# Bias products as row tiles, the small attention's softmax as one block, DMAs moved to ScalarE's queue, new instruction orders

## Chip, cores and metric

One core of a Trainium2 chip runs the kernel. The metric is the device time of one execution in microseconds (us); lower is better. TensorE (PE), VectorE (DVE), ScalarE (ACT), GpSimd (POOL) and SyncE (SP, which only issues DMAs here) each work through an instruction list of their own and meet at semaphores.

## The reference

Two transformer layers act on `x` of shape 64 x 64 x 256 (samples, rows of a sample, 256 features), with a context `ctx` of the same shape and a mask over the context's rows:

```python
x = x + L0_xattn(layernorm(x), ctx, Wq, bq, Wk, bk, Wv, bv, Wo, bo)     # 8 heads of 8 channels over 256 positions, rotary
x = x + L0_ffn(layernorm(x), gate_w, gate_b, val_w, val_b, out_w, out_b)
x = x + L1_xattn(layernorm(x), ctx, mask)                               # plain attention of 64 rows on 64 rows, no weights
x = x + L1_ffn(layernorm(x), w_gate_up, w_proj)
# L0_ffn: bit_linear(silu(bit_linear(x, gate_w) + gate_b) * (bit_linear(x, val_w) + val_b), out_w) + out_b;
#   bit_linear rounds each row to 8 bits and the weights to -1, 0, 1 times their mean magnitude
# L1_xattn: scores = x ctx^T / 16, masked, softmax, times ctx; rows of a sample with an all-masked context get 0
# L1_ffn: weights in groups of 64 rounded to -1, 0, 1 times the group's mean magnitude; silu(gate) * up, RMS norm, w_proj
```

In L0's attention the 64 rows of a sample are the channels, and the 256 features are the positions.

## The kernel before

**Pairs and stages.** Two samples are stacked to the 128 partitions; there are 32 such pairs. Every pair passes the same steps, named by short kinds. Projection stage (P): `xP`, `cP` (loads), `bsP mvP rsP xnP` (layer norm), `proj0 proj1` (query and key products), `pc r1 r2 rot` (rotary), `hi lo` (split into two fp16 parts), `kq` (six DMAs that lay the parts out in `KQ`, 32 partitions for each of four groups of heads), `v vst`. Attention (A): for each of 16 heads `S` (scores, TensorE, 31 rows), `mx` (row maximum, DVE), and, once all 16 maxima are there, `mxp` (TensorE transposes them), `mxc` (ACT copies them to `mxs`), `md` (a DMA writes them into row 31 of `KQ`), then for each head `T` (transposed scores minus maximum, TensorE, 32 rows), `E` (exponential, ACT) and, for each four heads, `pv`. `u ov sg rc d1 or om y x1` divide by the sum, project and add. FFN of L0 (B): `bsB mvB rsB xnB`, `amB sxB xr xq rq qT` (8-bit rounding and a DMA transpose), `Bg Bv` (two halves of 512 columns each), `tB aB hB amH sx hr hq ht Bd x2`. L1's attention (D): `bsD mvD rsD xnD xcT xcTc sc wx pD rs pT pTc ro x3`. FFN of L1 (C): `bsC mvC rsC xnC xh xl xT Cg Cu th aC hC sq hh hl hT Cd ms x4 st`.

**Order.** The steps run as a software pipeline. `ORDER` holds one written list for each engine; `S6:0` in iteration `it` is head 6 of pair `it + 0`, `Bg0:-3` works on pair `it - 3`, `proj0:2` on pair `it + 2`. An engine does its list in order, so a step that waits holds up all behind it. From the first step of a pair to its last are some ten iterations. Kinds in `ONCE` (the weights: `c ab ra qa rn cl qb fx tn tc` and `gm gv fr ct bs br mn val`) run once, in the iteration their number names, which puts them in the first iterations.

**PSUM.** `psS` and `psT` are two banks each for `S` and `T`, used in turn. Four more banks, `psW`, are shared by everything else: `BANKS` lists who takes each bank in turn, and `READER` names the step that must have read a bank before the next taker writes it. TensorE's `S` and `T` use row tiles: each works on the 32 partitions of its group, and four neighbours in the list are in four groups. `pv` uses column tiles, the rest the whole array.

**Places the change touches.** In `Bg` and `Bv` the bias is a third product into the same bank, of the whole array, from a 128-row tile `brow` with six rows that are not zero (L493). L960 (`wx`) takes the maximum and L657 (`pD`) the exponential of each sample's 64 x 64 block of the scores apart; L965 and L966 (`rs`, DVE) turn the sum into a factor. L732 and L737 on POOL centre and scale a row, among them `xnP`. SP issues every DMA: the weights (L299 to L320), and `md` (L350), which stands in SP's list after `kq` (L347), `cB`, `xT` (L390) and `hT` (L395, a DMA transpose that waits for `hl` of POOL):

```python
elif name == "md":
    after_apart(sp, "mxc", p)
    sp.dma_start(KQ[p % DEEP][31::32, 1, :, :], mxs[:]).then_inc(S["md"], 16)
```

Of the kernel before, what the change touches and what calls it, by code (L numbers as in the profile page):

```python
# [69 lines left out]
ORDER = {  # L70
    "pe": """Cd0:-7 tn4:-3 T4:-1 S6:0 S7:0 T5:-1 tn5:-3 pT:-5 Cd1:-7 ro:-5 pv0:-1 S8:0 T6:-1 T7:-1 S9:0 proj0:2 Bg0:-3
           T8:-1 S10:0 T9:-1 S11:0 pv1:-1 Bv0:-3 gm:0 tn1:-2 S12:0 S13:0 T10:-1 T11:-1 Bd:-4 Bg1:-3 S14:0 T12:-1
           S15:0 T13:-1 Bv1:-3 y:-2 proj1:2 mxp:0 T14:-1 S0:1 T15:-1 S1:1 pv2:-1 tn2:-2 Cg0:-5 pv3:-1 S2:1 T0:0 S3:1
           T1:0 xcT:-4 tn3:-2 tn0:-1 Cu0:-5 Cg1:-5 S4:1 T2:0 S5:1 T3:0 sc:-4 v:2 Cu1:-5""",
    "dve": """mx5:0 aC1:-6 bsP:3 cl1:-1 rc:-2 rs:-5 hC1:-6 ra2:1 mx6:0 x4:-7 mx7:0 ct1:-3 ct0:-2 x3:-5 mvP:3 ct2:-3
           bs:-1 ra1:2 mx8:0 mx9:0 bsC:-5 cl0:1 r1:2 mvC:-5 mx10:0 mx11:0 aB0:-3 mx12:0 mx13:0 val:1 fx2:-2 x2:-4
           hB0:-3 bsD:-4 mx14:0 mvD:-4 mx15:0 fx0:-1 gv:0 aB1:-3 bsB:-2 hB1:-3 mvB:-2 mx0:1 amH:-3 ra0:3 mx1:1
           fx1:-1 cl2:-1 sx:-3 mx2:1 mx3:1 aC0:-5 amB:-2 hC0:-5 sxB:-2 wx:-4 mx4:1""",
    "act": """th1:-6 pD:-5 xr:-3 pTc:-5 xq:-3 E4:-1 hh0:-6 E5:-1 tc4:-3 hi:1 hh1:-6 E6:-1 E7:-1 fr0:-1 fr2:-2 c1:21
           tc5:-3 tB0:-3 E8:-1 E9:-1 sq0:-6 E10:-1 xh:-5 E11:-1 ab2:0 ab0:1 u0:-1 tB1:-3 E12:-1 E13:-1 x1:-2 tc1:-2  # L80
           rn2:0 mxc:0 E14:-1 E15:-1 mn:1 pc:2 sq1:-6 c0:24 ab1:1 fr1:-1 th0:-5 tc2:-2 u1:-1 E0:0 hr0:-3 rn1:1 E1:0
           rn0:2 xcTc:-4 c2:4 hr1:-3 tc0:-1 tc3:-2 E2:0 E3:0 vst:2""",
    "pool": """rq:-3 ms:-7 rot:1 qa2:0 qa0:2 xb:-3 qb2:-2 hl0:-6 lo:1 rsC:-5 xnC:-5 qb0:-1 xl:-5 qa1:1 qb1:-1 om:-2
           hl1:-6 rsP:3 rsD:-4 xnD:-4 xnP:3 rsB:-2 xnB:-2 r2:2 hq0:-3 hq1:-3""",
    "sp": """xP:4 ov:-1 st:-7 cP:3 ht:-3 d1:-1 qT:-2 sm:3 or:-1 kq:2 br:0 cB:-3 w0:9 xT:-4 hT:-5 md:1 xA:0 sg:0""",
}
# [966 lines left out]
```

## Time and profile before

| | |
|---|---|
| time, median of 3 runs | 869.65 us (865.7 to 870.27) |
| the profiled execution's own time | 870.44 us |
| its span, first to last instruction | 868.6 us |
| busy in the span: PE, DVE, ACT, POOL | 757.4, 760.5, 687.1, 650.2 us (87, 88, 79, 75%) |
| granted TensorE clock, mean of the span | 0.935 of full |

Busy time is an average over a start, a long even part and an end. The start and the end have idle engines; what a step costs in the even part is read there, from the distance of one iteration's landmark to the next's. The landmark used below is `mxc` (L600), which runs once in each iteration.

### The profile page before, as it was taken

The page shows a single profiled execution, that of the slowest core. Times are in us where ns is not written, and L with a number is a line of the kernel's source. Part 1 is how long each engine was busy: PE and PEld are TensorE (multiplying, and loading weights), DVE is VectorE, ACT ScalarE, POOL GpSimd, SP SyncE. Part 2 cuts the span into 40 slices and gives each one's busy share as a digit, 9 for nine tenths or more (in the row PEclk, how much of TensorE's full clock was granted, in tenths as well). Part 3 has the DMA queues.
Part 4 walks back from the last instruction along what each step waited for, and adds up shares of the span by engine and source line. Part 5 has one row for each costly group of instructions (what it writes and reads, how often), then busy time and mean ns, then how long its engine had stood idle before and what let it go on. Part 6 is the DMA issues. An engine that isn't in the chain of part 4 may idle for free. (4 is left out here: it accounts for less than half of the span.)

```text
span 868.6 us, 21831 instructions
## 1 busy us (share of the span) xinstructions
PE 757.4 (87%) x6713; PEld 394.0 (45%) x6804; DVE 760.5 (88%) x1714; ACT 687.1 (79%) x1469; POOL 650.2 (75%) x1108
## 2 busy tenths in 40 slices
...
GB/s 327 70 38 27 51 68 75 70 102 101 96 112 97 100 108 106 104 105 111 108 104 105 101 110 105 104 106 104 101 96 112 97 102 96 92 81 105 83 43 72
DMA packets 210859, 84.67 MB, mean 97 GB/s; under 512 B 152748, under 2 KB 209708, under 8 KB 210744
## 3 DMA queue, kind: packets, MB, share of 16 engines
...
## 5 line engine op out<-in xcount | busy, mean ns | idle before, releaser
L876 DVE TENSOR_REDUCE mx<-psS 128x2 f32<-128x512 f32 x512 | 333.8, 679 | 26.6 <-PE psS L441 24.7
L595 ACT ACTIVATE prob<-psT 128x512 f32<-128x512 f32 x512 | 288.4, 603 | 32.1 <-PE psT L449 31.7
L441 PE MATMUL psS<-KQ 31*128 31x256 f16 x1024 | 132.7, 285 | 20.3 <-DVE mx L876 17.8
L463 PE MATMUL psW<-prob,vst 128*32 128x256 f32 x2048 | 143.4, 400 | 0.3 <-ACT prob L595 0.3
L528 PE MATMUL psW<-guT,xT 128*128 128x512 bf16 x482 | 124.4, 391 | 21.4 <-DMA xT<-stage 19.0
L449 PE MATMUL psT<-KQ 32*128 32x256 f16 x1024 | 113.4, 280 | 11.8 <-DMA KQ<-mxs 8.8
L776 POOL TENSOR_TENSOR stage<-stage 128x512 f16<-128x512 f32 x64 | 74.1, 1158 | 18.7 <-ACT stage L678 18.4
L441 PEld LDWEIGHTS psS<-KQ 31*128 31x128 f16 x1024 | 37.9, 93 | 103.4 <-DVE mx L876 77.3
L463 PEld LDWEIGHTS psW<-prob,vst 128*32 128x32 f32 x2048 | 55.0, 112 | 63.7 <-issue 32.4
L528 PEld LDWEIGHTS psW<-guT,xT 128*128 128x128 f16 x512 | 48.2, 100 | 74.9 <-issue 37.2
L762 POOL TENSOR_TENSOR hqB<-wide,rnd 128x512 bf16<-128x512 f32 x64 | 65.9, 1040 | 17.0 <-ACT wide L639 16.8
L490 PE MATMUL psW<-tern,xqT 128*128 128x512 bf16 x195 | 63.6, 382 | 16.4 <-DMA xqT<-xqB 10.7
L537 PE MATMUL psW<-pT,stage 128*128 128x256 bf16 x512 | 67.8, 278 | 5.2 <-DMA stage<-stage 5.2
L634 ACT ACTIVATE stage<-psW,sB 128x512 f32<-128x512 f32 x64 | 44.8, 701 | 31.5 <-PE psW L493 31.5
L537 PEld LDWEIGHTS psW<-pT,stage 128*128 128x128 f16 x512 | 50.2, 102 | 20.8 <-ACT vst L615 8.2
L977 DVE SCALAR_TENSOR_TENSOR stage<-stage,psW 128x512 f32<-128x512 f32 x64 | 43.6, 681 | 18.4 <-ACT stage L670 18.1
L670 ACT ACTIVATE stage<-psW 128x512 f32<-128x512 f32 x64 | 39.6, 619 | 21.1 <-PE psW L528 21.1
L449 PEld LDWEIGHTS psT<-KQ 32*128 32x128 f16 x1024 | 33.5, 93 | 50.1 <-issue 24.9
L476 PE MATMUL psW<-cP,wsm 128*128 128x256 f32 x128 | 46.7, 450 | 6.7 <-POOL xnP L737 4.6
L985 DVE SCALAR_TENSOR_TENSOR stage<-stage,hsc,psW 128x512 f32<-128x512 f32 x64 | 47.6, 743 | 3.1 <-PE psW L528 2.9
L493 PE MATMUL psW<-brow,xqT 128*128 128x512 bf16 x128 | 48.6, 380 | 0.1
L930 DVE SCALAR_TENSOR_TENSOR wide<-stage,psW 128x512 f32<-128x512 f32 x64 | 43.3, 677 | 5.3 <-ACT stage L634 5.3
...
## 6 DMA issues: line engine op xcount, KB each, us to landing
...
oR<-rden_d SPq DMA_DIRECT2D x128, 32.0 KB
...
```

The costliest lines, as they stand in the source:

```text
L441: m = nc.tensor.matmul(psS[:, n % 2, T * k:T * k + T], KQ[p % DEEP][r, 1, g, 128 * k:128 * k + 128], KQ[p % DEEP][r, 0, g, :], start=True, ...
L449: m = nc.tensor.matmul(psT[:, n % 2, T * k:T * k + T], KQ[p % DEEP][r, 0, g, 128 * k:128 * k + 128], KQ[p % DEEP][r, 1, g, :], start=True, ...
L463: m = nc.tensor.matmul(bank[32 * j:32 * j + 32, :], vst[p % DEEP][:, k, 4 * n + j, :], prob[:, (4 * n + j) % 8, k, :], start=(k == 0), sto ...
L490: nc.tensor.matmul(bank, xqT[:, k, :], (gT if kind == "Bg" else vT)[:, k, 512 * n:512 * n + 512], start=(k == 0), stop=False)
L493: m = nc.tensor.matmul(bank, xqT[:, NK, :], brow[:, int(kind == "Bv"), 512 * n:512 * n + 512], start=False, stop=True)
L528: m = nc.tensor.matmul(bank, xT[:, NK * part + k, :], w[:, k, :], start=(k == 0 and part == 0), stop=(k == NK - 1 and part == 1))
L537: m = nc.tensor.matmul(psW[:, BANK["Cd0"], 0:T], hT[:, 8 * part + c, :], pT[:, c, :], start=(c == 0 and part == 0), stop=(c == 7 and part ...
L595: m = nc.scalar.activation(flat(prob[:, n % 8, :, :]), psT[:, n % 2, :], ACT.Exp, scale=float(HC) ** -0.5)
L762: m = nc.gpsimd.tensor_tensor(hqB[:, h], hrB[:, h], rnd[:].broadcast_to([P, 512]), ALU.subtract)
L776: m = nc.gpsimd.tensor_tensor(hhl[:, 1, n, :], hC[:, n, :], hhl[:, 0, n, :], ALU.subtract)
L876: m = nc.vector.tensor_reduce(mx[:, p % 2, :, 4 * (n % 4) + n // 4], psS[:, n % 2, :].rearrange("p (c s) -> p c s", c=NK), AX.X, ALU.max)
L985: m = nc.vector.scalar_tensor_tensor(out=hC[:, n, :], in0=aC[:, n, :], scalar=hsc[:, 1:2], in1=psW[:, BANK[f"Cu{n}"], :], op0=ALU.mult, op ...
```

## The change

- `Bg` and `Bv` lose the third product. Four new steps, `bg0 bg1 bv0 bv1`, open their banks with the bias instead (six rows, row tiles of the four groups, 512 columns); `brow` now lies in groups at partitions 0, 32, 64, 96, and `rq` writes the row factors into four places.
- `sc` gets one more product (`own` and `other`, 2 rows, 128 columns) that pushes the two off-diagonal blocks far down; `wx` and `pD` then work on all 128 x 128 at once.
- `rs` moves from DVE to POOL (a power and a product). `xnP` moves from POOL (centre, scale) to ACT (one activation with scale and bias); POOL's `rsP` gains a product for the bias.
- `md` and the six 1 MB weight loads are issued from ACT's queue; each load has a semaphore of its own.
- POOL's weight products `qa`, `qb` run in four pieces each.
- `ORDER` and `BANKS` are new for all engines.

```diff
 ORDER = {
-    "pe": """Cd0:-7 tn4:-3 T4:-1 S6:0 S7:0 T5:-1 tn5:-3 pT:-5 Cd1:-7 ro:-5 pv0:-1 S8:0 T6:-1 T7:-1 S9:0 proj0:2 Bg0:-3
-           T8:-1 S10:0 T9:-1 S11:0 pv1:-1 Bv0:-3 gm:0 tn1:-2 S12:0 S13:0 T10:-1 T11:-1 Bd:-4 Bg1:-3 S14:0 T12:-1
-           S15:0 T13:-1 Bv1:-3 y:-2 proj1:2 mxp:0 T14:-1 S0:1 T15:-1 S1:1 pv2:-1 tn2:-2 Cg0:-5 pv3:-1 S2:1 T0:0 S3:1
-           T1:0 xcT:-4 tn3:-2 tn0:-1 Cu0:-5 Cg1:-5 S4:1 T2:0 S5:1 T3:0 sc:-4 v:2 Cu1:-5""",
+    "pe": """ro:-5 pv0:-1 T6:-1 S8:0 T7:-1 bg0:-3 S9:0 proj0:2 Bg0:-3 S10:0 T8:-1 T9:-1 S11:0 pv1:-1 Bd:-4 bv0:-3
+           S12:0 bv1:-3 S13:0 T10:-1 bg1:-3 T11:-1 Bv0:-3 Bg1:-3 Bv1:-3 S14:0 T12:-1 S15:0 T13:-1 y:-2 proj1:2 mxp:0
+           T14:-1 S0:1 S1:1 T15:-1 pv2:-1 Cg0:-5 pv3:-1 tn0:0 tn4:-4 Cg1:-5 xcT:-4 gm:1 S2:1 T0:0 S3:1 T1:0 Cu0:-5
+           v:2 sc:-4 S4:1 T2:0 S5:1 T3:0 tn2:-2 Cu1:-5 tn1:-1 tn3:-3 tn5:-4 Cd0:-6 pT:-4 S6:1 T4:0 S7:1 T5:0 Cd1:-6""",
...
     "act": (after)
+           ... mxc:0 E14:-1 E15:-1 md:0 pc:2 th0:-5 u1:-1 tc1:-2 xnP:3 rn1:1 tc0:0 th1:-5 xcTc:-4 E0:0 mn:3 E1:0 hr0:-3
+           vst:2 xr:-2 E2:0 pD:-4 c0:14 E3:0 xq:-2 hr1:-3 ab0:2 tc2:-2 c1:3""",
...
-    "sp": """xP:4 ov:-1 st:-7 cP:3 ht:-3 d1:-1 qT:-2 sm:3 or:-1 kq:2 br:0 cB:-3 w0:9 xT:-4 hT:-5 md:1 xA:0 sg:0""",
+    "sp": """xP:4 cP:3 st:-8 sm:9 ov:-1 d1:-1 qT:-2 ht:-3 or:-1 kq:2 xT:-4 cB:-3 xA:0 hT:-5 br:-1 sg:0""",
...
-BANKS = ("tn4 pT ro Bg0 tn1 Bg1 pv2 Cg1",
-         "Cd0 proj0 gm Bd Bv1 tn2 tn3 Cu0 v",
-         "pv0 y mxp Cg0 tn0 Cu1",
-         "tn5 Bv0 proj1 xcT sc")
+BANKS = ("bv1 tn0 Cg1 v tn1 tn5 Cd0",
+         "proj0 Bd y mxp Cg0 tn4 gm Cu1",
+         "ro bg0 bg1 pv2 Cu0 tn3",
+         "pv0 bv0 proj1 xcT sc tn2 pT")
...
+                    elif kind in ("bg", "bv"):
+                        after_dma(pe, "qT", p)
+                        if p == 0:
+                            after_dma(pe, "br", 0, 6)
+                        r = slice(32 * (2 * (kind == "bv") + n), 32 * (2 * (kind == "bv") + n) + 6)
+                        m = nc.tensor.matmul(bank, xqT[r, NK, :], brow[r, :], start=True, stop=False)
                     elif kind in ("Bg", "Bv"):
...
                         for k in range(NK):
-                            nc.tensor.matmul(bank, xqT[:, k, :],
-                                             (gT if kind == "Bg" else vT)[:, k, 512 * n:512 * n + 512],
-                                             start=(k == 0), stop=False)
-                        m = nc.tensor.matmul(bank, xqT[:, NK, :], brow[:, int(kind == "Bv"), 512 * n:512 * n + 512],
-                                             start=False, stop=True)
+                            m = nc.tensor.matmul(psW[:, BANK[f"{kind.lower()}{n}"], :], xqT[:, k, :],
+                                                 (gT if kind == "Bg" else vT)[:, k, 512 * n:512 * n + 512],
+                                                 start=False, stop=(k == NK - 1))
...
+                        m = nc.tensor.matmul(bank[:, 0:P], own[:], other[:], start=False, stop=True)
...
+            for i, (raw, part) in enumerate(((stage[:, 3, :], gu_w[0:HID, :]), (late[0], gu_w[HID:2 * HID, :]))):
+                nc.scalar.dma_start(raw.rearrange("p (r d) -> p r d", r=8), part.rearrange("(r p) d -> p r d", p=P))\
+                    .then_inc(S[f"w1_{i}"], 16)
+            ... (p_w, gate_wT, val_wT and out_wT in the same way)
...
+                    elif kind == "md":
+                        after(act, "mxc", p)
+                        nc.scalar.dma_start(KQ[p % DEEP][31::32, 1, :, :], mxs[:]).then_inc(S["md"], 16)
+                        continue
...
+                    elif kind == "xnP":
+                        after(act, "rsP", p)
+                        after(act, "proj", p - 1, 1)
+                        m = nc.scalar.activation(xnP[:], xP[:], ACT.Identity, scale=rsP[:, 1:2], bias=nmP[:])
...
-                        for b in range(2):
-                            h = slice(CH * b, CH * b + CH)
-                            m = nc.scalar.activation(pD[h, h], psW[h, BANK["sc"], h], ACT.Exp, bias=sD[h, 1:2],
-                                                     accum_out=sD[h, 2:3])
+                        m = nc.scalar.activation(pD[:], psW[:, BANK["sc"], 0:P], ACT.Exp, bias=sD[:, 1:2],
+                                                 accum_out=sD[:, 2:3])
...
+                        for g in range(0, WB // 64, 8):
+                            m = nc.gpsimd.tensor_tensor(q[:, g:g + 8, :], (w if kind == "qa" else q)[:, g:g + 8, :],
+                                                        by[:, g:g + 8, :], ALU.mult)
...
+                        if kind == "rsP":
+                            inner(2, m)
+                            m = nc.gpsimd.tensor_scalar(nmP[:], mv[:, 0:1], rs[:, 1:2], -1.0, ALU.mult, ALU.mult)
...
+                    elif kind == "rs":
...
+                        inner(1, nc.gpsimd.tensor_tensor(sD[:, 3:4], sD[:, 2:3], mone[:], ALU.pow))
+                        m = nc.gpsimd.tensor_tensor(sD[:, 4:5], sD[:, 3:4], valid[:, p:p + 1], ALU.mult)
...
-                        for b in range(2):
-                            h = slice(CH * b, CH * b + CH)
-                            m = nc.vector.tensor_reduce(sD[h, 1:2], psW[h, BANK["sc"], h], AX.X, ALU.max, negate=True)
+                        m = nc.vector.tensor_reduce(sD[:, 1:2], psW[:, BANK["sc"], 0:P], AX.X, ALU.max, negate=True)
```

## Rows read from the trace of the kernel before

**Rows 1.** Windows: start:end, length, busy (instructions) of each engine, clock, DMA share, GB/s.
```profile
250.00:700.00 450.00, 430.81 (x4080) 227.26 (x4137) 433.02 (x1017) 392.01 (x880) 378.34 (x665) 1.00 0.43 105
764.20:868.60 104.40, 72.67 (x474) 39.66 (x477) 54.53 (x134) 54.35 (x129) 62.73 (x120) 0.88 0.34 79
```

**Rows 2.** Tile `mxs`, then the timeline: start, length, instruction [idle before it, releaser].
```profile
L600 ACT ACTIVATE mxs<-psW x32: 373/373/374, 55.7 to 764.2; 16x256 f16<-16x256 f32 x32
...
145.12 0.37 ACT L600 ACTIVATE mxs<-psW 16x256 f16<-16x256 f32 x1 [0.61 <-PE psW L455]
...
443.47 0.37 ACT L600 ACTIVATE mxs<-psW 16x256 f16<-16x256 f32 x1 [0.61 <-PE psW L455]
...
467.78 0.37 ACT L600 ACTIVATE mxs<-psW 16x256 f16<-16x256 f32 x1 [0.61 <-PE psW L455]
...
490.06 0.37 ACT L600 ACTIVATE mxs<-psW 16x256 f16<-16x256 f32 x1 [0.61 <-PE psW L455]
...
764.19 0.37 ACT L600 ACTIVATE mxs<-psW 16x256 f16<-16x256 f32 x1 [0.48 <-PE psW L455]
```

**Rows 3.** Timeline of SP's queue beside two of those iterations.
```profile
442.93 2.85 SPq L395 DMA_TRANSPOSE stage<-stage  x1
445.82 0.63 SPq L350 DMA_DIRECT2D KQ<-mxs  x1
...
468.25 0.63 SPq L350 DMA_DIRECT2D KQ<-mxs  x1
```

**Rows 4.** Waits of TensorE, 250 to 700 us: total us, times, longest.
```profile
PE psT L449 <- DMA KQ<-mxs: 5.7, 8, 1.8
...
PEld psT L449 <- DMA KQ<-mxs: 8.7, 10, 2.1
```

**Rows 5.** DVE by line, 250 to 700 us (busy, mean ns | idle before), and its timeline.
```profile
L876 DVE TENSOR_REDUCE mx<-psS 128x2 f32<-128x512 f32 x315 | 205.9, 678 | 9.4 <-PE psS L441 8.6
...
L960 DVE TENSOR_REDUCE sD<-psW 64x1 f32<-64x64 f32 x38 | 8.2, 217 | 4.9 <-PE psW L512 4.4
...
752.08 0.11 DVE L965 RECIPROCAL sD<-sD 128x1 f32<-128x1 f32 x1
...
752.43 0.75 DVE L985 SCALAR_TENSOR_TENSOR stage<-stage,hsc,psW 128x512 f32<-128x512 f32 x1
```

**Rows 6.** Timeline of TensorE: a bias product, and a group of four tiles behind it.
```profile
412.36 0.38 PE L490 MATMUL psW<-tern,xqT 128*128 128x512 bf16 x1
412.58 0.38 PE L493 MATMUL psW<-brow,xqT 128*128 128x512 bf16 x1
412.89 0.28 PE L449 MATMUL psT<-KQ 32*128 32x256 f16 x1
...
413.23 0.42 PE L463 MATMUL psW<-prob,vst 128*32 128x256 f32 x4
```

**Rows 7.** Timeline of ACT: from the first softmax block to the next step.
```profile
406.60 0.30 ACT L657 ACTIVATE pD<-psW,sD 64x64 f32<-64x64 f32 x1
...
407.43 0.51 ACT L624 ACTIVATE xrB<-xnB,sB 128x256 f32<-128x256 f32 x1
```

**Rows 8.** Waits of ACT, 250 to 700 us.
```profile
ACT stage L634 <- PE psW L493: 18.9, 20, 1.9
```

**Rows 9.** POOL by line, 250 to 700 us.
```profile
L737 POOL TENSOR_TENSOR xnP<-ceP,rsP 128x256 f32<-128x256 f32 x20 | 12.3, 613 | 1.6
...
L724 POOL TENSOR_TENSOR rsD<-rsD,mhalf 128x1 f32<-128x1 f32 x20 | 11.0, 549 | 1.6
...
L722 POOL TENSOR_TENSOR rsC<-mvC,eps 128x1 f32<-128x1 f32 x20 | 3.8, 189 | 27.1 <-DVE mvC L897 27.1
```

**Rows 10.** Timeline of the start: SP's queue and DVE.
```profile
10.53 7.27 SPq L337 DMA_DIRECT2D xP<-in_x  x1
...
24.30 0.43 DVE L890 BATCH_NORM_STATS2 stP<-xP 128x6 f32<-128x256 f32 x1 [8.04 <-DMA xP<-in_x]
...
38.35 0.61 PE L441 MATMUL psS<-KQ 31*128 31x256 f16 x4 [1.65 <-DMA KQ<-hl]
```

More of the change, by code:

```diff
@@ L56 @@
 PARTS = {**{k: NH for k in ("S", "mx", "T", "E")}, "pv": NG,
-         **{k: 2 for k in ("proj", "u", "Bg", "Bv", "aB", "tB", "hB", "Cg", "Cu", "th", "aC", "hC", "sq",
+         **{k: 2 for k in ("proj", "u", "bg", "bv", "Bg", "Bv", "aB", "tB", "hB", "Cg", "Cu", "th", "aC", "hC", "sq",
                            "hh", "hl", "Cd", "hr", "hq")}}
 ONCE = {"c": 3, "ab": 3, "gm": 1, "gv": 1, "bs": 1, "br": 1, "mn": 1, "val": 1, "ra": 3, "qa": 3, "rn": 3, "cl": 3,
-        "qb": 3, "fx": 3, "fr": 3, "ct": 3, "tn": 6, "tc": 6, "w0": 1, "sm": 1}
+        "qb": 3, "fx": 3, "fr": 3, "ct": 3, "tn": 6, "tc": 6, "sm": 1}
 PARTS.update(ONCE)
-INNER = {"xnP": 1, "xnB": 1, "xnD": 1, "xnC": 1, "rsP": 1, "rsB": 1, "rsC": 1, "rsD": 1, "sxB": 1,
+INNER = {"xnB": 1, "xnD": 1, "xnC": 1, "rsP": 2, "rsB": 1, "rsC": 1, "rsD": 1, "sxB": 1,
          "sx": 2, "ms": 3, "rs": 1, "rq": 3, "rn": 1, "fr": 1, "ra": 3, "fx": 1, "gv": 4,
@@ L68 @@
 DEEP = 3
-SET_POOL, SET_DVE = 10, 2 * DEEP + 2
+SET_POOL, SET_DVE = 12, 2 * DEEP + 2
 ORDER = {
-    "pe": """Cd0:-7 tn4:-3 T4:-1 S6:0 S7:0 T5:-1 tn5:-3 pT:-5 Cd1:-7 ro:-5 pv0:-1 S8:0 T6:-1 T7:-1 S9:0 proj0:2 Bg0:-3
-           T8:-1 S10:0 T9:-1 S11:0 pv1:-1 Bv0:-3 gm:0 tn1:-2 S12:0 S13:0 T10:-1 T11:-1 Bd:-4 Bg1:-3 S14:0 T12:-1
-           S15:0 T13:-1 Bv1:-3 y:-2 proj1:2 mxp:0 T14:-1 S0:1 T15:-1 S1:1 pv2:-1 tn2:-2 Cg0:-5 pv3:-1 S2:1 T0:0 S3:1
-           T1:0 xcT:-4 tn3:-2 tn0:-1 Cu0:-5 Cg1:-5 S4:1 T2:0 S5:1 T3:0 sc:-4 v:2 Cu1:-5""",
[L75 to L84, printed above, removed]
-    "sp": """xP:4 ov:-1 st:-7 cP:3 ht:-3 d1:-1 qT:-2 sm:3 or:-1 kq:2 br:0 cB:-3 w0:9 xT:-4 hT:-5 md:1 xA:0 sg:0""",
-}
```

101 lines of the change are left out of this document (51 added, 50 removed).

## The prediction

> **What bounds the kernel now.** I first split the run by the landmark `mxc`. It runs first at 55.7 us, is at 145.12 in its fifth turn and at 764.19 in its last [rows 2]. From the fifth to the last are 27 iterations in 619.1 us, 22.93 us each. Ahead lie four iterations that also carry the weights' one-time work (89.4 us for the four), and behind the last landmark an end of 104.4 us [rows 1]. So 619 of 868.6 us are an even part, and what a change is worth is mostly 27 times what it does to the iteration.
>
> Second, who is busy in the even part. A window of 450 us holds 19.6 iterations (450 / 22.93). DVE is busy 433.0 / 19.6 = 22.1 us of each, PE 22.0, ACT 20.0, POOL 19.3 [rows 1]. Two engines are nearly full, at the full granted clock. PE's figure flatters, since modelled ends overlap; DVE's is what its instructions take.
>
> Third, whether iterations are alike. They are not: 443.47 to 467.78 is 24.31 us, 467.78 to 490.06 is 22.28 us [rows 2]. SP's queue tells them apart. `mxs` was written at 443.5, but its DMA (L350) was issued at 445.82, because SP sat in the transpose ahead of it (L395) from 442.93; in the good iteration the DMA went out at 468.25, half a us after `mxs` [rows 3]. The four groups of T0 cannot start without it: TensorE waited for this DMA 5.7 + 8.7 = 14.4 us in the window [rows 4], 0.73 us in each iteration, and TensorE's list is in order, so the next `S`, and through it DVE, wait too. The mean of 22.93 is thus 22.28 plus 0.65 of lateness. In the good iteration DVE is 99% busy: DVE, with PE close behind, is the floor, and the lateness of `md` is what lies on top.
>
> **The change, part by part, in us for each iteration.**
>
> *`md` on ACT.* It leaves the queue with `kq`, `xT` and `hT` ahead of it. In ACT's new list it stands behind E14 and E15, so it goes out some 1.5 us after `mxs`; but between `mxp` and T0 the new PE list has Cg1 and xcT as well as T14, S0, S1, T15, two `pv` and Cg0, so T0 comes later. I take off most of the lateness: 0.65 down to 0.2, since `kq`, `xT` and `hT` stay in one queue behind POOL. Bounds: 0 and 0.65.
>
> *PE.* A bias product of 512 columns takes 0.22 (412.36 to 412.58), four are 0.88. A group of four row tiles, eight products of 256 columns, takes 0.34 with the change of mode behind it (412.89 to 413.23) [rows 6]: its tiles run side by side. The new bias products have six rows and stand among such groups. `bg0` is in the partitions of S8 and follows it, 0.22. `bv0 S12 bv1 S13 T10 bg1 T11` put three of them beside the others: three of the four row groups have one bias more to do, and the run is longer by one, 0.22. So 0.88 becomes 0.44. The `own` product has a quarter of 512 columns: +0.06. Counting changes between whole array, row tiles and column tiles, the old list has 20 in an iteration and the new one 21 (Cg1 now stands behind pv3); one costs about 0.1, what 412.58 to 412.89 has above 0.22 [rows 6]. Net: -0.28. Bounds: all biases hidden, -0.72; no overlap, +0.16.
>
> The Trainium skill (TensorEngine Tiling (Array Packing), Key Properties) says that changing the tiling mode drains TensorE, which speaks against a list with more changes; the trace agrees, at about 0.1 each [rows 6]. By that rule alone the change would cost 0.1 an iteration; by the rows it is already in the sum.
>
> *DVE.* Two maxima of 64 columns take 217 ns each, 512 columns take 678 [rows 5], so a column costs 1.03 ns and one maximum over 128 takes 0.28 in place of 0.43: -0.15. `rs` goes: from L965 to the next step is 752.08 to 752.43 [rows 5], -0.35. Net -0.50. Bounds: the merged maximum no cheaper, -0.35; its wait for `sc` (4.4 us in the window, 0.22 each [rows 5]) gone as well, -0.72.
>
> *ACT.* The two softmax blocks with their accumulator reads take 0.83 (406.60 to 407.43) [rows 7]. One takes half, and its 64 more columns 0.07 (0.51 for 256 columns against 0.30 for 64 [rows 7]): -0.34. `xnP` is 0.51 by the row of the same size. The DMA issue takes SP 0.63 [rows 3]; ACT's queue isn't in the trace, so from 0 (E15 runs meanwhile) to 0.63. ACT goes from 20.0 to between 20.2 and 20.8, under the floor; I take 0.63 in full and find cover for it in ACT's 2.96 idle.
>
> *POOL.* Off go the two passes of `xnP`, 0.61 each, with a handover of 0.08 behind each (1.6 us over 20): -1.4. On come one small step in `rsP` and the two of `rs`: 0.19 + 0.19 + 0.55 [rows 9] and three handovers: +1.2. POOL stays at some 19.1 [rows 9], with 1.4 idle at `rsC` alone (27.1 us in the window). `rs` must be there for `x3` in the next iteration; beside it run `pT`, `pTc` and `ro`. The pieces of `qa` and `qb` are in the first iterations only. All this counts as nothing; if POOL's cover is gone, `hl` is late, then `hT`, then Cd0.
>
> *Start.* SP's issue of the second pair's `xP` lasted 7.27, from 10.53, behind the weights; it landed for DVE at 24.30 after 8.04 of waiting, and `r1` of the first pair stands behind that in DVE's list, so S0 came at 38.35 [rows 10]. With the weights on another queue this can shrink by up to 8. But the new ACT list has the mask row, two casts of weights, and now `xnP` itself ahead of the first rotary step, all in one queue, and `gm` stands ahead of S2 and waits for all three sums of ACT. I take -1, bounds -8 and +5.
>
> The Trainium skill (DMA: Bandwidth & Descriptors, Issuing engines are not separate DMA queues) holds that transfers of all issuing engines interleave on the same 16 DMA engines and that a second one saves only issue time. By it the 6 MB delay the second `xP` as before, and the start gains 0 to 1; that no load arrives sooner can't be read from the trace of before.
>
> *End.* Without `S` and `T` beside them the bias tiles need changes of mode of their own, four in three late iterations, +1; `rs` is longer but runs beside `ro`; no `md`. I take 0, bounds ±3.
>
> **Sum.** Floor of PE: 22.28 - 0.28 = 22.00. Floor of DVE: 22.28 - 0.50 = 21.78. The later one counts, 22.00, plus 0.2 of lateness: 22.2. That is 0.73 less than 22.93, times 27 = 19.7 us. With 1 from the start: 870.44 - 20.7 = 849.7. The profiled execution was 0.8 above the median of the runs, so the prediction is **849 us**.
>
> **Rivals.**
> - *Better than that:* no lateness, DVE's floor of 21.8, a start 5 shorter: 1.13 x 27 + 5 = 35.5, 834 us. For it: all three fullest places are relieved. Against: PE's new order has a mode change more. 9 in 100.
> - *The lateness stays:* SP's queue still holds `kq`, `hT` and `xT` in turn, so T4 or Cd0 takes T0's place; only PE's 0.28 counts: 0.28 x 27 = 7.6, 862 us. It needs `hT` to wait for POOL as at 442.93 [rows 3] and TensorE to have nothing else. 15 in 100.
> - *No change:* small gains eaten, for example by TensorE waiting at `bg0` for `x3` to free the bank of `ro`, with only pv0, T6, S8 and T7 between (before, proj0 too): 0.65 lost at this wait leaves the iteration at 22.9. 866 to 873 us. 10 in 100.
> - *Slower:* ACT becomes the bound. Its 20.8 of work plus today's idle of (450 - 392.0) / 19.6 = 2.96 make 23.76. A third of the idle is one wait for a product just being made (18.9 us in the window, 0.96 an iteration [rows 8]), which a denser list need not shorten, and `md` stands between two steps that feed TensorE. (23.76 - 22.93) x 27 = 22: 892 us at worst, about 880 if half the issue is covered. It decides once ACT's idle stays above 2.1. 14 in 100.
>
> The forecast itself, 838 to 860, gets 52 in 100.
>
> **Numbers.** What the measurement of this kernel can tell from no change is about 0.5%, 4.3 us. Faster by more: forecast, better, and lateness stays, 0.76. Within: 0.10. Slower: 0.14. The range takes the better case's 834, and at the top goes past no change to 872; it leaves out the slower case and the far end of the start's bounds.
>
> **What would show it.** Right: landmarks 22.0 to 22.4 apart with no long ones among them; waits of T0 for `KQ<-mxs` near nothing; DVE near 21.6 of work an iteration; row-tile bias products starting within 0.05 of their neighbours; ACT under 21. Wrong: a new long wait of TensorE (`bg0` on `x3`, S0 on `kq`, Cd0 on `hT`), ACT idle still near 3 with landmarks above 22.9, or a first landmark after 60 us.

## The result, and the profile after

The changed kernel takes **856.31 us** (median of four runs, 853.29 to 858.92), the kernel before 869.86 beside it: a ratio of 0.985, 95% interval 0.981 to 0.990. That is faster by 13.6 us, where the forecast was 20.7. The profiled execution took 853.29 us, with a span of 851.4.

Head of the page, then two windows of the kernel after: start:end, length, busy time and instructions of PE, PEld, DVE, ACT and POOL, granted clock, DMA share, GB/s; they answer to [rows 1].
```profile
span 851.4 us, 22001 instructions
...
PE 750.5 (88%) x6836; PEld 395.3 (46%) x6836; DVE 740.3 (87%) x1618; ACT 695.6 (82%) x1437; POOL 647.9 (76%) x1160
...
250.00:700.00 450.00, 442.64 (x4335) 239.38 (x4332) 443.38 (x1000) 415.71 (x899) 393.67 (x713) 1.00 0.48 109
...
750.00:851.40 101.40, 69.98 (x431) 36.92 (x430) 46.75 (x107) 48.00 (x110) 62.16 (x120) 0.86 0.35 75
```

The landmark `mxc` of the kernel after, by its tile and by ACT's timeline. It answers to [rows 2]; the fifth is at 148.56.
```profile
L595 ACT ACTIVATE mxs<-psW x32: 373/373/374, 60.1 to 744.2; 16x256 f16<-16x256 f32 x32
...
148.56 0.37 ACT L595 ACTIVATE mxs<-psW 16x256 f16<-16x256 f32 x1 [0.61 <-PE psW L441]
...
392.63 0.37 ACT L595 ACTIVATE mxs<-psW 16x256 f16<-16x256 f32 x1
...
414.58 0.37 ACT L595 ACTIVATE mxs<-psW 16x256 f16<-16x256 f32 x1
...
744.25 0.37 ACT L595 ACTIVATE mxs<-psW 16x256 f16<-16x256 f32 x1
```

| part of the span | before | after | difference | forecast |
|---|---|---|---|---|
| up to the first landmark | 55.7 | 60.1 | +4.4 | -1 for both |
| the first four iterations | 89.4 | 88.4 | -1.0 | |
| the 27 even ones | 619.1 | 595.7 | -23.4 | -19.7 |
| behind the last landmark | 104.4 | 107.15 | +2.7 | 0 |
| span | 868.6 | 851.4 | -17.2 | -20.7 |

(The profiled executions differ by more than the medians, 17.2 against 13.6; each is read against its own kind.) The even part gained more than forecast, and start and end gave 6 us back. An iteration is now 22.06 us (595.7 / 27), against 22.93. Its median is 21.95, as 392.63 to 414.58 shows, against 22.28 in a good iteration before. So of the 0.65 us of lateness 0.11 are left (0.54 x 27 = 14.6 us), and the floor, the length of an iteration that nothing holds up, is 0.33 lower (0.33 x 27 = 8.9 us). The window now holds 450 / 22.06 = 20.4 iterations: DVE is busy 21.7 us in each, PE 21.7, ACT 20.4, POOL 19.3. ACT is idle 1.7 by this count, which leaves out the issuing of DMAs: `md`'s, some 0.55, lies in those 1.7.

TensorE's waits of the kernel after from 250 to 700 us (us in total, times, longest). `KQ<-mxs` of [rows 4] doesn't appear at all; what is new is a wait of `pT` (L504) for `pD`, 14.8 us or 0.7 in each iteration.
```profile
PEld psS L427 <- DVE mx L897: 21.9, 55, 0.5
...
PEld psW L504 <- ACT pD L658: 9.8, 18, 0.7
...
PE psW L504 <- ACT pD L658: 5.0, 15, 0.5
```

Timeline of the kernel after: `md` (ACTq, L598) goes out 0.45 after `mxs`, 0.2 **ahead** of the transpose of `hT` (SPq, L381); T0 (L435) follows 4.2 later with no wait. In [rows 3] the transpose stood ahead of `md`. Over the 20 iterations of the window `md` goes out 0.45 to 0.98 after `mxs` (the prediction had 1.5), and ahead of the transpose in 19. It lands 1.9 to 4.0 us after its issue. T0 comes 4.2 to 4.3 after the issue, against 2.3 to 2.8 in the iterations of before without a wait, so the longer way to T0 is used too: six of the 20 landings came later than 2.8.
```profile
393.08 0.56 ACTq L598 DMA_DIRECT2D KQ<-mxs  x1
393.29 2.64 SPq L381 DMA_TRANSPOSE stage<-stage  x1
...
397.24 0.28 PE L427 MATMUL psS<-KQ 31*128 31x256 f16 x1
397.25 0.28 PE L435 MATMUL psT<-KQ 32*128 32x256 f16 x1
```

Timeline of TensorE, kernel after: the bias products (L474, six rows) among row tiles, to be read beside [rows 6].
```profile
409.98 0.39 PE L474 MATMUL psW<-brow,xqT 6*128 6x512 bf16 x1
409.98 0.28 PE L427 MATMUL psS<-KQ 31*128 31x256 f16 x1
409.99 0.38 PE L474 MATMUL psW<-brow,xqT 6*128 6x512 bf16 x1
...
410.20 0.27 PE L435 MATMUL psT<-KQ 32*128 32x256 f16 x1
410.22 0.38 PE L474 MATMUL psW<-brow,xqT 6*128 6x512 bf16 x1
...
410.59 1.47 PE L479 MATMUL psW<-tern,xqT 128*128 128x512 bf16 x6
```
Two bias products start within 0.01 us of each other and of a product of `S`. The group with three of them lasts 0.61 us (409.98 to 410.59), against 0.34 for one without [rows 6]: the three cost 0.27 together, where three products over the whole array cost 0.66 before.

Groups of instructions of the kernel after, 250 to 700 us (total and mean ns of one, then idle before it).
```profile
L979 DVE TENSOR_REDUCE sD<-psW 128x1 f32<-128x128 f32 x20 | 5.3, 266 | 0.0
...
L643 ACT ACTIVATE xnP<-xP,nmP,rsP 128x256 f32<-128x256 f32 x20 | 12.0, 602 | 0.0
L658 ACT ACTIVATE pD<-psW,sD 128x128 f32<-128x128 f32 x20 | 7.2, 358 | 0.0
L658 ACT ACTIVATION_READ_ACCUMULATOR pD<-psW,sD 128x1 f32 x20 | 4.0, 199 | 0.0
...
L805 POOL TENSOR_TENSOR sD<-sD,mone 128x1 f32<-128x1 f32 x20 | 11.0, 549 | 0.0
```
These are new shapes, and each can be set against its estimate: 266 ns for the merged maximum (0.28), 0.36 + 0.20 for the merged softmax (0.49), 0.60 for `xnP` (0.51), 0.55 for POOL's power (0.55, as its like in [rows 9]).

Start of the kernel after, to be read beside [rows 10]: SP's queue, the first step of ACT that needs the mask row (L573), the second pair's statistics (L911), and the first `S`.
```profile
7.71 10.76 SPq L319 DMA_DIRECT2D mrow<-in_mask  x1
19.21 5.88 SPq L319 DMA_DIRECT2D mrow<-in_mask  x1
25.13 8.71 SPq L326 DMA_DIRECT2D xP<-in_x  x2
...
26.77 1.91 ACT L573 ACTIVATE mneg<-mrow 2x2048 bf16<-2x2048 uint8 x1 [14.46 <-DMA mrow<-in_mask]
27.49 0.43 DVE L911 BATCH_NORM_STATS2 stP<-xP 128x6 f32<-128x256 f32 x1 [12.72 <-DMA xP<-in_x]
...
42.86 0.61 PE L427 MATMUL psS<-KQ 31*128 31x256 f16 x4 [2.90 <-DMA KQ<-hl]
```
The two small mask rows now hold SP's queue for 16.6 us (3.9 and 1.3 before), ahead of the second pair's `xP`; ACT waits 14.46 for them. The first `S` comes 4.5 us later than before, and so does the first landmark.

### The profile page after: what moved, and what is told of

Same layout as the page of the kernel before. It is cut to its first block and busy times, and to the rows that moved or that the text cites. A ratio compares the mean times of both kernels' runs of the same rounds, so it can differ in the third digit from the quotient of the medians.

```text
span 851.4 us, 22001 instructions
## 1 busy us (share of the span) xinstructions
PE 750.5 (88%) x6836; PEld 395.3 (46%) x6836; DVE 740.3 (87%) x1618; ACT 695.6 (82%) x1437; POOL 647.9 (76%) x1160
## 5 line engine op out<-in xcount | busy, mean ns | idle before, releaser
L897 DVE TENSOR_REDUCE mx<-psS 128x2 f32<-128x512 f32 x512 | 331.1, 678 | 15.1 <-PE psS L427 14.3
L516 PE MATMUL psW<-guT,xT 128*128 128x512 bf16 x512 | 135.5, 390 | 13.6 <-DMA xT<-stage 11.9
L427 PE MATMUL psS<-KQ 31*128 31x256 f16 x1024 | 129.1, 284 | 12.7 <-DVE mx L897 9.3
L435 PE MATMUL psT<-KQ 32*128 32x256 f16 x1024 | 119.8, 279 | 3.2 <-ACT prob L590 2.2
L516 PEld LDWEIGHTS psW<-guT,xT 128*128 128x128 f16 x512 | 41.2, 99 | 84.8 <-issue 52.2
L776 POOL TENSOR_TENSOR hqB<-wide,rnd 128x512 bf16<-128x512 f32 x64 | 66.5, 1040 | 14.3 <-ACT wide L638 14.3
L479 PE MATMUL psW<-tern,xqT 128*128 128x512 bf16 x256 | 68.5, 392 | 0.0
L462 PE MATMUL psW<-cP,wsm 128*128 128x256 f32 x128 | 47.4, 455 | 22.3 <-DMA cP<-in_ctx 19.1
L990 DVE SCALAR_TENSOR_TENSOR stage<-stage,psW 128x512 f32<-128x512 f32 x64 | 43.6, 682 | 21.3 <-ACT stage L671 20.2
L633 ACT ACTIVATE stage<-psW,sB 128x512 f32<-128x512 f32 x64 | 44.0, 688 | 20.1 <-PE psW L479 18.5
L435 PEld LDWEIGHTS psT<-KQ 32*128 32x128 f16 x1024 | 40.9, 93 | 33.3 <-ACT prob L590 20.5
L604 ACT COPY uA<-psW 128x512 f32<-128x512 f32 x64 | 37.5, 586 | 21.7 <-PE psW L449 21.7
L770 POOL TENSOR_TENSOR r<-pc,tab 128x512 f32<-128x512 f32 x32 | 40.7, 1272 | 17.3 <-ACT pc L609 17.3
```

The lines of the kernel that those rows point to most:

```text
L427: m = nc.tensor.matmul(psS[:, n % 2, T * k:T * k + T], KQ[p % DEEP][r, 1, g, 128 * k:128 * k + 128], KQ[p % DEEP][r, 0, g, :], start=True, ...
L435: m = nc.tensor.matmul(psT[:, n % 2, T * k:T * k + T], KQ[p % DEEP][r, 0, g, 128 * k:128 * k + 128], KQ[p % DEEP][r, 1, g, :], start=True, ...
L462: m = nc.tensor.matmul(bank[:, T * f:T * f + T], wqk[:, j, :], (cP, xnP)[f][:], start=True, stop=True)
L479: m = nc.tensor.matmul(psW[:, BANK[f"{kind.lower()}{n}"], :], xqT[:, k, :], (gT if kind == "Bg" else vT)[:, k, 512 * n:512 * n + 512], sta ...
L516: m = nc.tensor.matmul(bank, xT[:, NK * part + k, :], w[:, k, :], start=(k == 0 and part == 0), stop=(k == NK - 1 and part == 1))
L633: m = nc.scalar.activation(tB[:, 512 * n:512 * n + 512], psW[:, BANK[f"bg{n}"], :], ACT.Tanh, scale=sB[:, p % 2, 4:5])
```

## The experiments

Each was run beside the kernel before on the same chip; ratios are to it. `b_slack`, `a_md_sp_early`, `a_pt_late` and `a_start` ran on another chip than the rest, where the kernel before took 867.68 us (869.63 and 869.95 in the other two groups), so they are compared with the others by ratios as well. Landmark figures are distances over the 27 even iterations of the profiled execution, the mean where nothing else is said. A second run of the changed kernel, in the first group, gave the level for comparisons: 856.47 us, 0.985 (0.981 to 0.990), mean 22.15. Its expectation:

> The changed kernel once more, as the yardstick of this group on the same chip. Both theories: 853 to 859 us. Its landmarks (the copy of the maxima, once an iteration) were 21.95 us apart in the undisturbed iterations, 22.06 in the mean; the time moved between 853 and 859 from run to run, and the profile of this run may show where.

### Which part of the move takes the lateness away

**`md` on ACT alone, in the kernel before** (`b_md_act`).
```diff
-  E14:-1 E15:-1 mn:1           (ACT)       xT:-4 hT:-5 md:1 xA:0   (SP)
+  E14:-1 E15:-1 md:0 mn:1      (ACT)       xT:-4 hT:-5 xA:0        (SP)
```


> The kernel before, with one thing changed: the DMA of the maxima is issued from ACT's queue, behind E15. Theory 1 (the DMA was late because of what stood ahead of it in SP's queue, 0.65 us an iteration): landmarks 22.3 apart with none over 22.7, waits of T0 for it down from 14.4 us in the window 250 to 700 to under 7 (the old list has less work between the maxima and T0 than the new one, so some stays), time 853 to 860. Rival A (SP's queue and POOL hold up the iteration in another place, and this DMA only shows it): landmarks stay near 22.9, time 865 to 873. Rival B (the issue of 0.6 us on ACT costs what it saves): T0's wait gone, but the landmarks evenly at 22.7 or more.

868.8 us, 0.999 (0.995 to 1.002): nothing. The mean distance is 22.92. `md` now always leaves 0.41 us after `mxs` begins, and T0 still waits for it. Timeline and waits of this kernel:
```profile
352.13 2.18 SPq L392 DMA_TRANSPOSE stage<-stage  x1
...
353.27 0.37 ACT L597 ACTIVATE mxs<-psW 16x256 f16<-16x256 f32 x1 [0.61 <-PE psW L452]
...
353.68 0.55 ACTq L600 DMA_DIRECT2D KQ<-mxs  x1
...
358.22 0.28 PE L446 MATMUL psT<-KQ 32*128 32x256 f16 x1 [1.36 <-DMA KQ<-mxs]
```
```profile
PEld psT L446 <- DMA KQ<-mxs: 8.3, 9, 1.6
...
PE psT L446 <- DMA KQ<-mxs: 5.8, 9, 1.4
```
The waits are 14.1 us, before 14.4 [rows 4]. `md` no longer stands behind the transpose in a queue, but in 19 of the window's 20 iterations it is still issued after it, here by 1.55 us, and it lands 4.5 us after its issue. This run refutes my reason: taking away the time that `md` spends in SP's queue is not enough.

**One entry moved in the list of the kernel before** (`b_md_first`). `md` stays on SP, ahead of the transpose.
```diff
-  w0:9 xT:-4 hT:-5 md:1 xA:0 sg:0
+  w0:9 xT:-4 md:1 hT:-5 xA:0 sg:0
```


> The kernel before with one entry of SP's list moved: the DMA of the maxima stands ahead of the transpose hT and not behind it, as it goes out in the changed kernel. Theory 2 (a DMA that is issued once hT is under way lands late, one issued ahead of it does not): it lands about 2 us after its issue, T0's waits for it go from 14.4 us to under 4 in the window 250 to 700, landmarks 22.3 to 22.6 in the mean, time 855 to 864. Rival (the long iterations also come from the transposes themselves, xT ahead of Cg0 and xqT ahead of Bg0, which this leaves as they are): T0's waits gone, landmarks still 22.7 or more, 865 to 870.

**856.19 us**, 0.985 (0.979 to 0.990): as much as the whole change. Timeline:
```profile
394.14 0.37 ACT L600 ACTIVATE mxs<-psW 16x256 f16<-16x256 f32 x1 [0.61 <-PE psW L455]
...
394.54 0.62 SPq L350 DMA_DIRECT2D KQ<-mxs  x1
395.28 1.61 SPq L395 DMA_TRANSPOSE stage<-stage  x1
...
397.36 0.28 PE L449 MATMUL psT<-KQ 32*128 32x256 f16 x1
```
T0 starts 2.8 us after `md`'s issue, and it waits for `md` in only one of the window's 20 iterations. The even part falls by 12.4 us, to a mean of 22.47 with a median of 22.28: the floor of before, unchanged, and most of the lateness gone.

I looked at the order of issue in every iteration of the window. In the kernel before, the transpose of `hT` was issued 1.5 to 3.5 us ahead of `md` in all 20, and where T0 waited, it started 3.9 to 6.0 us after that transpose's issue, whether `md` had left 0.4 or 2.4 after `mxs`. In `b_md_act` that was 4.0 to 6.1. The other transpose, of `xT`, was issued 1.4 to 3.2 us ahead of `md` in `b_md_first` too, and held up nothing.

The DMA packets in the traces show where the time goes. In `b_md_act` `md` has a queue of its own in the trace (q10), so its 16 packets can be told apart. They started 1.2 to 2.0 us after the issue in nine of the ten iterations in which T0 didn't wait for them. In the five with the longest waits (262.49, 353.27, 445.33, 513.17, 676.41) they started 2.8 to 3.6 us after it, when at most 8 of the transpose's packets of 256 bytes were still to come: they had stood behind the transfer, though not behind the issue.

In the kernel before there are seven iterations in which `md` went out within 0.51 us of `mxs`, and T0 waited in five of them. In all five one transfer of 16 KB, of a kind that the profile calls `instruction`, began 1.1 to 1.4 us after `md`'s issue, where `md`'s own packets begin (1.3 to 1.4), and `md` landed 3.5 to 3.9 us after its issue; in four of the five, four or more of its packets took 1.4 to 1.6 us each, and otherwise 0.03. In the other two (375.6 and 467.78) there was no such transfer, and `md` landed after 2.2 us. Kernel before, DMA view of 513.3 to 517.0, with a wait, then of 468.2 to 470.4, without (queue, kind: packets, MB, share of the 16 engines):
```profile
q1 hardware_dynamic: 1809, 0.55, 90.4%
q8 instruction: 1, 0.02, 1.6%
...
q1 hardware_dynamic: 1758, 0.49, 102.3%
```
Such a transfer alone isn't enough: in two more iterations of before (535.98 and 696.7) one began 1.2 to 1.5 us after `md`'s issue, and `md` landed in time. In `b_md_first` `md` landed after 1.8 us in 18 of 20 iterations, and the one wait again had such transfers at 1.34 and 1.42. This is read from what coincides in time; no run here takes those transfers away.

**`md` back on SP in the changed kernel**, behind `hT` (`a_md_sp`) and ahead of it (`a_md_sp_early`); ACT's list loses its `md:0`.
```diff
-  cB:-3 xA:0 hT:-5 br:-1 sg:0
+  cB:-3 xA:0 hT:-5 md:1 br:-1 sg:0        a_md_sp
+  cB:-3 xA:0 md:1 hT:-5 br:-1 sg:0        a_md_sp_early
```


> The changed kernel, with the DMA of the maxima back in SP's queue behind the transpose hT. Theory 1: it is late again in part of the iterations; the new TensorE list has 2 us more work ahead of T0, so only the worst are felt: landmarks 22.2 to 22.6, time 861 to 872. Rival (the new order alone took the wait away, the queue doesn't matter): within 3 us of the changed kernel, and ACT, without the issue, a little emptier.

> The changed kernel with the DMA of the maxima in SP's queue, but ahead of the transpose hT (the run with it behind hT took 876 us). Theory 2: the place before hT is what counts, not the queue; it goes out within 1 us of the maxima as on ACT, and hT is only held until then: 856 to 862 us, landmarks 21.95 to 22.2. Rival (the queue counts: SP is full, and a wait for the maxima in it holds up xT, hT and the rest): 866 us or more, with new waits for xT, hT or KQ<-hl.

Behind: 876.35 us, 1.007 (1.004 to 1.010), mean 22.89. `md` leaves 2.4 to 4.4 us after `mxs`, and T0 waits 43.6 us in the window:
```profile
PEld psT L438 <- DMA KQ<-mxs: 24.3, 18, 2.6
...
PE psT L438 <- DMA KQ<-mxs: 19.3, 18, 2.3
```
Ahead: 858.21 us, 0.989 (0.983 to 0.995), mean 22.27, median 21.96, which the measurement can't tell from the changed kernel. `md` leaves 0.4 to 1.5 us after `mxs`, and T0, 3.6 to 4.4 after that, never waits. Which queue it is makes no difference that can be told; the side of the transpose makes 16 us by the ratios, 18 by the times. And the longer way to T0 in the changed kernel (4.6 us from `mxs`, 3.2 in `b_md_first`) doesn't save a late `md`.

**More work ahead of T0, in the kernel before with `md` on ACT** (`b_slack`).
```diff
-  pv3:-1 S2:1 T0:0 S3:1 T1:0 xcT:-4 tn3:-2 tn0:-1 Cu0:-5 Cg1:-5 S4:1
+  pv3:-1 Cg1:-5 xcT:-4 S2:1 T0:0 S3:1 T1:0 tn3:-2 tn0:-1 Cu0:-5 S4:1
```


> The kernel before with the DMA of the maxima on ACT's queue and, in TensorE's list, Cg1 and xcT moved ahead of S2, so that T0 comes some 1.6 us later after the maxima. Theory 2 (what is late is the DMA's landing: up to 4.4 us after its issue while the transpose hT is under way, whichever queue issues it; only more work ahead of T0 hides it): T0's waits for it under 2 us in the window 250 to 700, landmarks 22.2 to 22.5, 852 to 860 us. Rival (T0's wait is a symptom; the long iterations come from another chain through POOL and the transposes): T0's waits gone, yet landmarks still 22.7 or more with long ones of 24 among them, 863 to 872 us.

923.13 us, 1.064 (1.058 to 1.070), mean 24.64. T0's waits are gone, but Cg1 takes a bank that ACT hasn't read yet:
```profile
PEld psW L525 <- ACT uA L606: 21.3, 18, 1.2
...
PE psW L525 <- ACT uA L606: 12.7, 18, 0.7
```
A new wait took the place of the old, so this run says nothing on the lateness. It shows that two steps moved by hand can cost 1.7 us an iteration.

### The floor: bias tiles, DVE's work, PE's work

**Bias products over the whole array again** (`a_bias_full`), each beside whole-array neighbours.
```diff
-  T6:-1 S8:0 T7:-1 bg0:-3 S9:0 ...  S12:0 bv1:-3 S13:0 T10:-1 bg1:-3 T11:-1 Bv0:-3
+  T6:-1 S8:0 T7:-1 S9:0 bg0:-3 ...  bv1:-3 S12:0 S13:0 T10:-1 T11:-1 bg1:-3 Bv0:-3
-  matmul(bank, xqT[r, NK, :], brow[r, :], start=True, stop=False)
+  matmul(bank, xqT[:, NK, :], brow[:, int(kind == "bv"), 512 * n:512 * n + 512], start=True, stop=False)
```


> The changed kernel, with the four bias products over the whole array (six rows that are not zero in 128), each beside other whole-array products so that no change of mode is added. Theory 1 (TensorE and DVE are both at their limit, the row tiles save 0.44 us of TensorE an iteration): landmarks up by 0.3 to 0.45, time up by 9 to 14 us, 865 to 870. Rival (DVE alone is the limit and TensorE has room): landmarks up by under 0.15, time up by less than 5 us.

862.2 us, 0.991 (0.989 to 0.994), median distance 22.28, mean 22.42. The tiles are worth 5.7 us, 0.33 in the median iteration.

**`rs` on DVE again, two softmax blocks, no own product** (`a_dve_back`).
```diff
-  mx6:0 x4:-7 bsP:3 x3:-5          (DVE)      rq:-2 rs:-4    (POOL)
+  mx6:0 x4:-7 bsP:3 rs:-5 x3:-5    (DVE)      rq:-2          (POOL)
-  tensor_reduce(sD[:, 1:2], psW[:, BANK["sc"], 0:P], AX.X, ALU.max, negate=True)
+  for b in range(2): tensor_reduce(sD[h, 1:2], psW[h, BANK["sc"], h], AX.X, ALU.max, negate=True)
```


> The changed kernel with the small attention as before: rs on DVE ahead of x3, the maxima and exponentials of the two 64 x 64 blocks apart, no own product. DVE has 0.5 us more work an iteration, ACT 0.3 more, POOL 0.9 less, TensorE 0.06 less. Theory (DVE, 98.5% busy, sets 21.95): landmarks 22.3 to 22.5, 866 to 871 us. Rival (TensorE sets it and DVE has room): landmarks under 22.1, 856 to 860.

882.69 us, 1.015 (1.010 to 1.020), with a median of 22.89 between landmarks (mean 23.02): 0.94 more, where 0.5 of DVE's work had been put back. Window and waits:
```profile
250.00:700.00 450.00, 426.41 (x4077) 229.57 (x4136) 438.99 (x1020) 409.86 (x902) 363.60 (x643) 1.00 0.47 104
```
```profile
PEld psW L503 <- ACT pD L659: 16.5, 20, 1.2
...
PE psW L503 <- ACT pD L659: 11.4, 19, 0.9
```
The wait of `pT` for `pD` has grown from 14.8 to 27.9 us. DVE is less full than in the changed kernel (439.0 of 450, against 443.4), so it isn't DVE's work alone. A chain through it that has become longer would fit; this run doesn't show the chain.

**Less work on one engine.** `a_light_dve` takes the four layer-norm statistics over 64 of 256 columns; `a_light_pe` leaves the second half of the contraction out of `Bg` and `Bv`.
```diff
-  m = nc.vector.bn_stats(st[:], src[:])
+  m = nc.vector.bn_stats(st[:], src[:, 0:64])              a_light_dve
-  for k in range(NK):
+  for k in range(1):                                       a_light_pe
```


> The changed kernel with DVE lighter: the four row statistics read 64 of the 256 columns (so the layer norms use statistics of a quarter of the row), about 0.2 us less for each, 0.8 us of DVE an iteration. If DVE alone sets the iteration: landmarks near 21.2, time 833 to 838. If TensorE is as full as DVE: landmarks 21.6 to 21.9, 846 to 855, and TensorE's waits for mx gone. If DVE is no limit at all: no change, 856.

> The changed kernel with TensorE lighter: Bg and Bv leave out the second half of their contraction, four products of 512 columns, 0.88 us of TensorE an iteration. If TensorE alone sets the iteration: landmarks near 21.1, time 831 to 838. If DVE is as full as TensorE: landmarks 21.6 to 21.9, 846 to 855, with TensorE idle for mx. If TensorE is no limit: no change, 856.

854.28 us, 0.984 (0.978 to 0.989), and 853.21, 0.982 (0.978 to 0.987), beside 0.985 for the changed kernel. The medians of the distance are 21.90 and 21.75 us, against 21.95. (The means are 22.05 and 22.18, against 22.06: in `a_light_pe` four iterations were over 23 us.) The windows, DVE's first, then PE's:
```profile
250.00:700.00 450.00, 435.19 (x4273) 239.56 (x4331) 430.63 (x1001) 415.24 (x899) 393.86 (x717) 1.00 0.48 109
```
```profile
250.00:700.00 450.00, 425.71 (x4189) 231.01 (x4254) 440.42 (x1000) 411.12 (x900) 393.94 (x714) 1.00 0.48 109
```
Relieved by 12.8 us (DVE) or 16.9 us (PE) in the window, 0.6 to 0.8 in an iteration, the kernel gives back 0.05 (DVE) and 0.20 (PE) in the median. Neither engine's work alone sets 21.95. What is taken off becomes idle time on that engine.

**`pT` later, to take away its wait for `pD`** (`a_pt_late`).
```diff
-  Cd0:-6 pT:-4 S6:1 T4:0 S7:1 T5:0 Cd1:-6
+  Cd0:-6 S6:1 T4:0 S7:1 T5:0 pT:-4 Cd1:-6
```


> The changed kernel with pT one place later in TensorE's list, behind T5 instead of ahead of S6. In the changed kernel TensorE waits there for pD, 14.8 us in the window 250 to 700, 0.7 us an iteration. Theory (TensorE is at its limit, so this wait is on the path): landmarks down from 21.95 to 21.6 or 21.7, time 845 to 852. Rival (DVE, busy 98.5% of the window, holds the iteration at 21.95, and TensorE's wait is free): 855 to 858, landmarks 21.9 to 22.1.

864.02 us, 0.995 (0.992 to 0.998): the wait is gone, and the kernel is **slower**, by 7.5 us as the times stand and 9 by the ratios (median distance 22.06, mean 22.39). TensorE now waits for the exponentials at L435 instead (14.3 us in the window, before the move 8.6). Taking the wait away by this move gains nothing. That the wait is free isn't shown by it, since the move also puts off everything that follows `pT`: `pTc`, `ro` and `x3`.

### The start

**The small loads (`sm`: biases, mask, the two mask rows) behind the second pair's load** (`a_start`), in the changed kernel.
```diff
-  st:-8 sm:9 ov:-1    (SP)     E0:0 mn:3 E1:0    (ACT)     mx0:1 val:2 amH:-3    (DVE)
+  st:-8 sm:2 ov:-1    (SP)     E0:0 mn:0 E1:0    (ACT)     mx0:1 val:0 amH:-3    (DVE)
```


> The changed kernel with the small loads (biases, mask, mask row) two iterations into SP's list, behind the second and third pair's, and the mask row's conversion and the mask's reduction in iteration 0. In the changed kernel SP sat 10.8 and 5.9 us in the issues of the mask rows, ACT waited 14.5 us for them and DVE 12.7 us for the second pair's x. Theory (that is why its first landmark is at 60.1 and not at 55): first landmark at 48 to 55, all later distances unchanged, time 845 to 851. Rival (the weights on the other queue hold back the second x anyway): first landmark 58 or later, 854 to 858.

**845.65 us**, 0.976 (0.971 to 0.981), the fastest of all: 22.0 us below the kernel before beside it (867.68), and 10.8 below the changed kernel's 856.47 on the other chip (8 by the ratios). The even part has the same median, 21.96. The first landmark comes at 50.2:
```profile
12.03 9.42 SPq L326 DMA_DIRECT2D xP<-in_x  x2
...
17.91 0.43 DVE L911 BATCH_NORM_STATS2 stP<-xP 128x6 f32<-128x256 f32 x1 [3.43 <-DMA xP<-in_x]
...
24.50 1.74 SPq L319 DMA_DIRECT2D mrow<-in_mask  x1
...
33.50 0.61 PE L427 MATMUL psS<-KQ 31*128 31x256 f16 x4 [5.70 <-DMA KQ<-hl]
...
L595 ACT ACTIVATE mxs<-psW x32: 356/372/373, 50.2 to 737.9; 16x256 f16<-16x256 f32 x32
```
A mask row issued at 24.50 takes 1.74, and 10.76 when issued at 7.71. The two issues of `xP` are long here too, 9.42 together. The second pair's statistics run 9.6 us earlier than in the changed kernel, and 6.4 earlier than before [rows 10].

## Why the prediction was right, and where it was off

**Direction and range held; two thirds of the gain came.** 856 us lies within 834 to 872, and faster had 0.76. Between the landmarks the numbers were close: 22.06, where 22.2 was forecast, and from 250 to 700 us no iteration is longer than 22.3 (one of 23.04 lies ahead of it). That the lateness went as forecast is partly luck, as the next paragraph shows.

**The lateness: right effect, wrong reason.** I put 0.65 down to the time that `md` spends behind the transpose in SP's queue, and expected 0.2 to stay because `kq`, `xT` and `hT` share that queue still. 0.11 stayed. But taking `md` off the queue alone gave nothing (`b_md_act`), and giving it a place ahead of the transpose in the same queue gave 13.4 us (`b_md_first`). What counts is that `md` is issued before the transpose of `hT`; that the new lists do so was no part of my reasoning. In [rows 3] both readings fit, and I took the one that the timeline draws, an issue behind an issue; and I had looked at two iterations. Five of the seven in which `md` went out promptly waited all the same, and what told them from the good one was a transfer on another DMA queue, which SP's queue doesn't show. The Trainium skill (DMA: Bandwidth & Descriptors, Issuing engines are not separate DMA queues) holds that DMAs of all issuing engines run on the same DMA engines and interleave, and that issuing from several saves only the time of the issue. The trace agrees with the second half: `b_md_act` saved the time in SP's queue, and the waits stayed at 14.1 us. Of interleaving it shows both: in the iteration at 422.33 `md`'s packets moved among the transpose's, and in the five with the longest waits only behind nearly all of them.

**PE's term: right in size.** -0.28 was the sum; PE's busy time fell from 22.0 to 21.7 in an iteration, and the floor by 0.33. The tiles run beside their neighbours as worked out (0.27 for a group of three against 0.22), and putting them back costs 0.33 in the median iteration, against the 0.44 of work that I had for them. Whether PE's work sets the floor is another matter; the light runs speak against it.

**DVE's term: the model was wrong, though the sum was near.** I let the later of two floors count, PE's 22.00 or DVE's 21.78. By the light runs neither floor is what sets 21.95, and by `a_dve_back` DVE's 0.50 is worth 0.94. My reading is that both engines, with ACT at 20.4 between them, form chains, in which work added to a link shows in full or more and work taken off one link shows hardly; which chain it is, the runs don't settle, since the edits of `a_dve_back` were made together, so `rs` ahead of `x3` and the two blocks aren't told apart. DVE's busy time itself fell by 0.34, from 22.07 to 21.73, since one small step of it became 0.24 longer (L942, last section); without that the -0.50 would have been met.

**ACT: cost a little low, rival refuted.** 20.4 of work without the issue and 0.55 for the issue make 20.9, just above the 20.8 that I had as the most; `xnP`, 0.60 for 0.51, and the softmax, 0.56 for 0.49, account for it. The rival was to decide once ACT's idle stayed above 2.1; it fell from 2.96 to 1.7, since the wait at L634 of [rows 8], 18.9 us, has shrunk to 1.6 (now L633).

**No change through `bg0`: refuted.** At the bias products (L474) TensorE waits for `x3` 0.6 us in the whole window. The largest new wait, for `pD`, could not be turned into time (`a_pt_late`).

**The start: the step that failed.** I took -1 with bounds of -8 and +5, and got +3.4 up to the fifth landmark. I named the mask row among what stood ahead of the first rotary step, but gave it no price of its own, and kept the hope that the second `xP` would get out sooner without the weights in its queue. In place of them stood two mask rows whose issue took 16.6 us while the weights were loading from ACT's queue. `a_start` shows both: with the rows later, the first landmark comes 9.9 us earlier than after and 5.5 earlier than before, and the fifth, at 136.7, 8.4 earlier than before. So the gain I had bounded at -8 was there, more than the 0 to 1 that I had set beside it, and the place of `sm` in SP's list hid it.

**The end:** +2.7, inside the ±3 given it, and not taken apart. Start and end together turn 23.4 us into 17.2, and that is why a one-entry edit of the old kernel equals the whole change: `b_md_first` has 606.6 in the even part, 11 more than the changed kernel, but a start of 56.0 and an end of 105.0.
